# Other slots for the attention steps, a second output buffer in x1, identity products in the first block, and another order in the last block

## What is computed

```python
x = hidden_states
n = layernorm(x)
q, k, v = n @ Wq.T, n @ Wk.T, n @ Wv.T
# chunks of 64 rows: o = q @ state + tril(q @ k.T) @ v; state = state + k.T @ v
o = o / max(|sum(q * cumsum(k))|, 1)
o = rmsnorm(o) * norm_w
x = x + layernorm(o @ Wo)
n = layernorm(x)
w = routing(sigmoid(n @ Wr / temperature))     # zone weights, else the two nearest experts
y = sum over e of w[e] * ((silu(n @ Wg[e]) * (n @ Wu[e])) @ Wd[e])
out = x + layernorm(y)
```

## Time and profile before

| | |
|---|---|
| time, three runs | 1609.62, 1609.85, 1610.92 us; median 1609.85 |
| profiled execution | 1609.45 us, its span 1607.7 us |
| busy | PE 94%, DVE 62%, ACT 43%, POOL 28% |
| mean granted clock of TensorE | 0.983 |
| one pass of the loop | 96.2 us, from one wait of `kv 1` to the next |
| a store of 256 KB, from issue to landing | 2.2 us (median) |

### The profile page before, as it was taken

The page is one execution under the profiler, slowest core; times in us unless marked ns, Lnnn a source line. Parts: engine busy times, 40 slices in busy tenths (PEclk is TensorE's granted clock), DMA queues, the critical chain, the costliest instruction groups (busy, mean ns, idle before and its releaser), DMA issues. The chain is left out here.

```text
span 1607.7 us, 35519 instructions
## 1 busy us (share of the span) xinstructions
PE 1514.8 (94%) x13504; PEld 1299.3 (81%) x13504; DVE 989.7 (62%) x2388; ACT 692.4 (43%) x1264; POOL 456.4 (28%) x720
## 2 busy tenths in 40 slices
PE   5599999999999999999999999999999999999987
PEld 4488888788888888888788888888888888888876
DVE  5546666666665666656666665666656666665654
ACT  4443534444343443434444343443444445343432
POOL 1322413224241232413224241233413224241220
PEclk9599999999999999999999999999999999999999
DMA  3300000000000000000000000000000000000000
GB/s 113 98 2 3 25 0 13 13 13 13 0 13 13 13 13 12 14 0 13 13 13 13 0 13 13 13 13 13 13 0 13 13 13 13 0 13 15 1 14 13
DMA packets 25342, 24.54 MB, mean 15 GB/s; under 512 B 2016, under 2 KB 25056, under 8 KB 25312
## 3 DMA queue, kind: packets, MB, share of 16 engines
q1 hardware_dynamic: 25312, 24.13, 4.7%
HBM read 15.74 MB, written 8.39 MB: 15 GB/s over the span
## 5 line engine op out<-in xcount | busy, mean ns | idle before, releaser
L899 DVE TENSOR_TENSOR late<-late,up_ps 128x512 f32<-128x512 f32 x256 | 175.4, 685 | 317.7 <-PE up_ps L412 288.3
L412 PE MATMUL down_ps<-w_hi,h_hi 128*128 128x256 f32 x976 | 266.7, 295 | 0.0
L704 ACT ACTIVATE late<-gate_ps 128x512 f32<-128x512 f32 x256 | 152.7, 597 | 235.6 <-PE gate_ps L412 235.6
L412 PE MATMUL down_ps<-w_hi,h_lo 128*128 128x256 f32 x976 | 253.5, 281 | 0.0
L623 ACT ACTIVATE h_hi<-late 128x512 fp32r<-128x512 f32 x256 | 160.6, 627 | 203.5 <-DVE late L899 203.5
L1093 POOL TENSOR_TENSOR rms_f<-rms_in,minus_half 128x16 f32<-128x16 f32 x32 | 93.7, 2929 | 511.0 <-DVE rms_in L863 511.0
L919 DVE SCALAR_TENSOR_TENSOR late<-down_ps,route,late 128x256 f32<-128x256 f32 x364 | 158.1, 476 | 112.7 <-PE down_ps L412 109.2
L412 PE MATMUL gate_ps<-ft_hi,w_hi 128*128 128x512 f32 x512 | 211.3, 413 | 6.1 <-ACT late L704 5.3
L815 DVE TENSOR_TENSOR h_lo<-late,h_hi 128x512 fp32r<-128x512 f32 x256 | 175.2, 684 | 59.3 <-ACT h_hi L623 59.3
L412 PE MATMUL up_ps<-ft_hi,w_hi 128*128 128x512 f32 x512 | 204.2, 399 | 0.0
L412 PE MATMUL up_ps<-ft_hi,w_lo 128*128 128x512 f32 x512 | 204.0, 398 | 0.0
(11 more groups left out here) (154 smaller groups left out, 2638.1 us busy)
## 6 DMA issues: line engine op xcount, KB each, us to landing
xs<-in_x SPq DMA_DIRECT2D x32, 256.0 KB, 2.9
out_rows<-late SPq DMA_DIRECT2D x32, 256.0 KB, 2.2
late<-in_wg SPq DMA_DIRECT2D x8, 256.0 KB, 3.0
late<-in_wu SPq DMA_DIRECT2D x8, 256.0 KB, 2.8
late<-in_wd SPq DMA_DIRECT2D x8, 256.0 KB, 2.8
late<-in_wkv_t SPq DMA_DIRECT2D x1, 512.0 KB, 5.6
late<-in_wq_t SPq DMA_DIRECT2D x1, 256.0 KB, 4.4
late<-in_wo_t SPq DMA_DIRECT2D x1, 256.0 KB, 5.5
```

The source lines that it names most:

```text
L412: last = nc.tensor.matmul(dst, lhs, rhs, start=n == 0, stop=n == len(terms + low_terms) - 1)
L704: nc.scalar.activation(h_f[:, m, :], gate_ps[:, :], ACT.Silu).then_inc(silu_ready[0], 1)
L899: nc.vector.tensor_tensor(h_f[:, m, :], h_f[:, m, :], up_ps[m][:, :], ALU.mult).then_inc(h_ready[0], 1)
```

## The change

It moves steps among the slots of `STEPS`: `kv 1` from slot 5 to 3, `o 0` and `su 1` from 8 to 7, `norm_stats 0` from 9 to 8, `s 1` from 10 to 8, `norm_apply 0` from 11 to 10, `o 1` from 12 to 11, `ot 0` from 13 to 12, `ln2_apply 0` from 17 to 16, `ln2_add 0` and `ln3_stats 0` from 18 to 17, `ln2_stats 1` from 19 to 18, `ln3_apply 0` from 20 to 19, `ft 0` and `ln2_apply 1` from 21 to 20, `ln2_add 1` and `ln3_stats 1` from 22 to 21, `ln3_apply 1` from 24 to 23, `ft 1` from 25 to 24. The others stay. The second half's outputs go to a buffer of their own, which lies in `x1`. `normalise_x` signals each of its four tiles. In the first block TensorE makes products of the identity into `gate_ps` ahead of steps, and the order of the start on ScalarE and VectorE differs. In the last block `keep_x1`, `normalise_out` of the block before, the wait for its `out_add` and the last but one `add_down`s stand elsewhere.

```diff
--- before.py
+++ after.py
@@ -56,22 +56,21 @@
     [("xt", 0), ("xt", 1)],
     [("kv", 0)],
     [("q", 0), ("q", 1)],
-    [("kt", 0)],
+    [("kv", 1), ("kt", 0)],
     [("su", 0), ("s", 0)],
-    [("kv", 1), ("keep_x1",)],
+    [("keep_x1",)],
     [("kt", 1)],
+    [("o", 0), ("su", 1)],
+    [("norm_stats", 0), ("s", 1)],
     [],
-    [("o", 0), ("su", 1)],
-    [("norm_stats", 0)],
-    [("s", 1)],
     [("norm_apply", 0)],
     [("o", 1)],
-    [("ot", 0), ("norm_stats", 1)],
+    [("ot", 0)],
+    [("norm_stats", 1)],
     [("wo", 0)],
     [("norm_apply", 1), ("ln2_stats", 0)],
-    [("ot", 1)],
-    [("wo", 1), ("ln2_apply", 0)],
-    [("ln2_add", 0), ("ln3_stats", 0)],
+    [("ot", 1), ("ln2_apply", 0)],
+    [("wo", 1), ("ln2_add", 0), ("ln3_stats", 0)],
     [("ln2_stats", 1)],
     [("ln3_apply", 0)],
     [("ft", 0), ("ln2_apply", 1)],
@@ -79,6 +78,7 @@
     [],
     [("ln3_apply", 1)],
     [("ft", 1)],
+    [],
     [("ft_out", 0), ("ft_out", 1)],
     [],
 ]
@@ -109,6 +109,9 @@
     [("ft_out", 1)],
     [],
 ]
+
+FIRST_WARM = {("kv", 0): 4, ("s", 0): 1, ("kv", 1): 2, ("s", 1): 3, ("o", 1): 4, ("ot", 0): 4, ("wo", 0): 5, ("ot", 1): 5,
+              ("wo", 1): 4, ("ft", 0): 10, ("ft", 1): 14}
 ROUTER = ("r",)
 
 
@@ -159,11 +162,14 @@
         o_n = shared[:, :].rearrange("p (a b h d) -> p a b h d", a=2, b=2, h=H)
         fin = shared[:, :].rearrange("p (t n) -> p t n", t=TILES)
         state = sb("state", [P, B, 4, 2, HG * PAIR])
-        o_sb = sb("o_sb", [P, 2, H, VA])
+        o_sb0 = sb("o_sb0", [P, 2, H, VA])
         o_sq = sb("o_sq", [P, 2, H, VA])
 
         ot_hi, ot_lo = (xt[:, 0, :].rearrange("p (b n) -> p b n", b=B) for xt in (xt_hi, xt_lo))
         x1 = sb("x1", [P, TILES, HID])
+
+        o_sb = [o_sb0[:, :, :, :], x1[:, :, :].rearrange("p t n -> p (t n)")[:, 0:2 * H * VA]
+                .rearrange("p (b h v) -> p b h v", b=2, h=H)]
 
 
         ft_hi, ft_lo = sb("ft_hi", [P, KT, TOK], f32r), sb("ft_lo", [P, KT, TOK], f32r)
@@ -216,7 +222,7 @@
         x_loaded = counter("x_loaded", 32)
         out_stored = counter("out_stored", 32, 32)
         att_done = counter("att_done", N_PSUM)
-        xn_ready = counter("xn_ready", 1)
+        xn_ready = counter("xn_ready", TILES)
         xt_hi_ready = counter("xt_hi_ready", KT)
         xt_ready = counter("xt_ready", KT)
         q_ready = counter("q_ready", HG)
@@ -425,8 +431,11 @@
                     reach(pe, count, (a[0], a[1] - 1), k)
                 if kind == "xt":
                     k = step[1]
-                    reach(pe, xn_ready, a, 1)
                     for t in range(TILES):
+                        if psum_order(a) is FIRST_PSUM_STEPS:
+                            reach(pe, xn_ready, a, t + 1)
+                        elif t == 0:
+                            reach(pe, xn_ready, a, TILES)
                         last = nc.tensor.transpose(dst[:, t // 2, t % 2 * P:t % 2 * P + P], rows[:, t, k * P:k * P + P],
                                                    ident[:, :])
                 elif kind == "q":
@@ -488,7 +497,8 @@
                                                             start=False, stop=b == B - 1 and j == HPG - 1)
                 elif kind == "su":
                     p = step[1]
-                    reach(pe, v_ready, a, p + 1)
+                    if psum_order(a)[number - 2][0] != "kv":
+                        reach(pe, v_ready, a, p + 1)
                     pe.sem_inc(quarters_begun, 1)
                     for b in range(B):
                         for g in range(HG):
@@ -587,12 +597,23 @@
                 up(0, 1, a)
                 down(E - 1, 1, f)
 
+
+
+            def warm(count):
+                for _ in range(count):
+                    nc.tensor.matmul(gate_ps[:, 0:P], ident[:, :], ident[:, :], start=True, stop=True)
+
             pe.wait_ge(const_ready, 1)
+            warm(14)
             for n, steps in enumerate(FIRST_STEPS):
-                if n == 1:
-                    pe.wait_ge(w_ready, ATT_W)
                 for step in steps:
+                    warm(FIRST_WARM.get(step, 0))
+                    if step == ("kv", 0):
+                        pe.wait_ge(w_ready, 2)
+                    if step == ("wo", 0):
+                        pe.wait_ge(w_ready, ATT_W)
                     att_step(step, (0, 0))
+            warm(2)
             pe.wait_ge(w_ready, ATT_W + 3)
             up(0, 0, (0, 0))
             pe.wait_ge(wr_ready, 1)
@@ -631,7 +652,8 @@
                 return last
 
             def normalise_x(a):
-                ln_apply(1, 1, a, rows, xs, range(TILES), shift1, rstd1).then_inc(xn_ready[0], 1)
+                for t in range(TILES):
+                    ln_apply(1, 1, a, rows, xs, [t], shift1, rstd1).then_inc(xn_ready[0], 1)
 
             def normalise_out(p, f):
                 ln_apply(4, p + 1, f, fin, fin, range(2 * p, 2 * p + 2), shift4, rstd4).then_inc(fin_ready[0], 1)
@@ -656,14 +678,14 @@
                     last.then_inc(kz_ready[0], 1)
                 elif kind == "o":
                     p = step[1]
-                    reach(act, on_ready, a, p)
+                    reach(act, on_ready, a, p - 1)
                     for i in range(2):
-                        last = copy(o_sb[:, :, i * HPG:i * HPG + HPG, :],
+                        last = copy(o_sb[p][:, :, i * HPG:i * HPG + HPG, :],
                                     src[:, i, :].rearrange("p (b j v) -> p b j v", b=B, j=HPG))
                     last.then_inc(o_copied[0], 1)
                     reach(act, rms_in_ready, a, p)
                     reach(act, o_copied, a, p + 1)
-                    nc.scalar.activation(o_sq[:, :, :, :], o_sb[:, :, :, :], ACT.Square).then_inc(o_squared[0], 1)
+                    nc.scalar.activation(o_sq[:, :, :, :], o_sb[p], ACT.Square).then_inc(o_squared[0], 1)
                 elif kind == "ot":
                     copy(ot_hi, src).then_inc(ot_hi_ready[0], 1)
                 elif kind == "wo":
@@ -766,9 +788,11 @@
 
             act.wait_ge(att_w_loaded[0], 16)
             copy(wq_hi[:, :, :], wq_raw).then_inc(w_hi_ready, 1)
+            normalise_x((0, 0))
             act.wait_ge(att_w_loaded[1], 16)
             copy(wkv_hi[:, :, :], wkv_raw).then_inc(w_hi_ready, 1)
-            normalise_x((0, 0))
+            for step in FIRST_STEPS[0]:
+                att_step(step, (0, 0))
             act.wait_ge(wo_scaled, 1)
             copy(wo_hi[:, :, :], wo_raw).then_inc(w_hi_ready, 1)
             act.wait_ge(small_loaded, 48)
@@ -776,8 +800,9 @@
             copy(wr_h0[:, :, 0:E], wr_raw[:, :, :])
             nc.scalar.activation(wr_h0[:, :, E:2 * E], wr_raw[:, :, :], ACT.Copy, scale=0.0).then_inc(wr_hi_ready, 1)
             for n, steps in enumerate(FIRST_STEPS):
-                for step in steps:
-                    att_step(step, (0, 0))
+                if n > 0:
+                    for step in steps:
+                        att_step(step, (0, 0))
                 high_of_unit(n)
             act.wait_ge(temp_ready, 1)
             act.wait_ge(w_ready, ATT_W + UNITS - 2)
@@ -794,12 +819,15 @@
                 first_expert((i, 1), (i, 0), (i, -1))
             rest((BLOCKS - 1, 0), (BLOCKS - 2, 0), more=False)
             f = (BLOCKS - 1, 0)
-            first_expert(None, f, (BLOCKS - 2, 0))
-            keep_x1(f)
+            first_expert(None, f, None)
             for e in range(2, E):
                 for m in range(MT):
                     silu(e, m, f)
                     high(e, m, f)
+                if e in (3, 4):
+                    normalise_out(e - 3, (BLOCKS - 2, 0))
+                if e == 6:
+                    keep_x1(f)
             normalise_out(0, f)
             normalise_out(1, f)
 
@@ -865,7 +893,7 @@
                 elif kind == "norm_apply":
                     p = step[1]
                     reach(dve, rms_ready, a, p + 1)
-                    nc.vector.tensor_tensor(o_n[:, p, :, :, :], o_sb[:, :, :, 0:D],
+                    nc.vector.tensor_tensor(o_n[:, p, :, :, :], o_sb[p][:, :, :, 0:D],
                                             rms_f[:, p, :, :].unsqueeze(3).broadcast_to([P, B, H, D]), ALU.mult)\
                         .then_inc(on_ready[0], 1)
                 elif kind == "ot":
@@ -912,6 +940,8 @@
             def add_down(e, p, f):
                 if e == 1:
                     reach(dve, acc_scaled, f, p + 1)
+                if e == E - 1 and is_last(f):
+                    reach(dve, down_read, f, 2 * (e - 2) + p + 1)
                 reach(dve, down_done, f, 2 * e + p + 1)
                 for n in range(2):
                     t, src = 2 * p + n, down_bank(e, p, f)[:, n * HID:(n + 1) * HID]
@@ -970,15 +1000,17 @@
             x_stats((0, 0))
             nc.vector.memset(state[:, :, :, :, :], 0.0)
             settle(nc.vector.memset(v_sb[:, :, :, D:VA], 1.0))
+            dve.wait_ge(w_hi_ready, 1)
```

(17 more changed lines are left out.)

## The result

The changed kernel takes 1562.61 us (median of 4 runs, 1561.69 to 1563.77), the kernel before 1609.93 (4 runs, 1609.62 to 1610.92): a ratio of 0.9705, 95% interval 0.9689 to 0.9722. That is 47.3 us less; 45.4 were forecast.

A forecast was written before the change was run, and what follows sets the result against it. TensorE, busy 94% of the span, can gain only where it stands still or runs at half clock. Loop 33, first block 3 and last block 9 us sum to 45: 1609.85 - 45.4 = 1564.4, own range 1558 to 1570.

The forecast's parts named there:

- The stretch from `kt 1` to `down(1,1)`: Loop: a new TensorE wait of 1.0 to 1.2 us in each pass that finishes an output.
- the `state` wait: Loop: TensorE's wait ahead of kv 1 for DVE's state sums, 1.96 us from start to start, goes.
- Rival (b): Loop: no new wait replaces kv 1's, DVE or GpSimd being quicker than summed; 59 us gained, 1550; chance 0.14.
- `ft`: Loop: waits ahead of the two ft transposes shrink, 1.1 to 1.3 of 2 x 0.65 us gained a pass.
- rival (c): Loop: the new wait takes kv 1's whole gain, or ft keeps its waits; 1579, half way 1572; chance 0.24.
- The pass: Loop: one pass gains 2.3 us (2.0 to 2.5) and takes 93.9.
- Rival (d): Loop: slower, keep_x1 waiting on ScalarE for the store and delaying silu(2,1); 1627 if the store takes 10 us; chance 0.03.
- The first block: Block 1's predecessor: own output buffer and identity products gain 3 us, bounds 1 and 5.
- The buffer: First block: the o 1 copy and following square leave the way of ot 0's copy; about 1.1 us, bounds 0.7 and 1.7.
- The clock held through `up(0,0)`: First block: identity products may keep full clock, 2.9 us instead of 5.25, gaining 2.3; half was given.
- The 1.4 at `kv 0`: First block, kv 0: a further 1.4 us may come from the clock, at the same odds as at up(0,0).
- The last block: Last block: up(3,0) 7.5 us earlier, the tail 1.5 to 1.8; total 9.2, bounds 7.7 and 10.

The follow-up runs named there:

- `kv_only`: The changed kernel with the loop's slots of before, except kv 1 alone moved from slot 5 to slot 3: 1583.09 us, ratio 0.9841.
- `norm_first`: The changed kernel with ScalarE issuing normalise_out(1) ahead of the k and v copies of kv 1: 1548.49 us, ratio 0.9629.
- `no_products`: The changed kernel without any identity product: 1564.56 us, ratio 0.9736.
- `norm_early_last`: The changed kernel with the last block's normalise_out, and so out_add, back in first_expert, keep_x1 left at expert 6: 1562.95 us, one run.

## Why the prediction was right, step by step

**The stretch from `kt 1` to `down(1,1)`.** Forecast: the `state` wait goes (1.96) and a wait on `add_down(1,0)` of 1.0 to 1.2 comes, for 0.9 to 1.1 gained a pass. Measured: the new wait costs 1.05, and `kv_only` gains 12.6 us, 0.9 in each of 14 passes. `norm_first` shows the cause: with `normalise_out(1)` ahead the wait is gone and 14.7 us with it. Rival (b), no wait, is what that kernel does and the changed one doesn't. One number was written down wrong: DVE's wait for GpSimd was to grow to "near 3.5 or more", while the text's own shift (298.4 against 295.14, on top of 1.74) makes 5.0; 4.86 was measured.

**`ft`.** Forecast: 1.1 to 1.3 a pass, `ft 1` with nothing to spare. Measured: all waits gone in the loop, 20.3 us, 1.35 in each of the 15 blocks that have them. The doubt was too large: `ft 1` starts at 344.80 behind an `ln3_apply` that runs from 342.99 to 344.1, 0.7 to spare. With that, rival (c) falls. The pass came out at 94.0 (93.9 forecast).

**Rival (d), the store.** `keep_x1` waits 0.8 us at most in the loop, and nothing of it reaches TensorE. The price was rightly placed, though: in the last block, where no slack lies behind it, it was 68.4 - 62.5 = 5.9 us.

**The first block.** Forecast 3, measured 4.0: 0.9 up to `ft 1` and 3.2 from there to `xt`. The buffer gave its 1.1 between `ot 0` and `ot 1` (8.31 before, 7.22 after), of which 0.9 is left at `ft 1`. The clock held through `up(0,0)`, where I had given it even odds: 5.25 went to 2.87, all of the 2.3 forecast in that case; of the 3.2, 2.4 are the products' by `no_products` and 0.8 came without them. The 1.4 at `kv 0`, also at even odds, did not come in this profile: `kv 0` took 4.42 (4.20 before), while it took 2.9 in four of the nine profiles with products at the start. So the 3 was a mean of outcomes, and that the profile gave 4.0 is in part luck. The clock behind `ft 1` does not always hold either: in 3 of the 10 profiles with products ahead of it the stretch took 12.6 to 13.2 us instead of 11.4. It was 11.4 in all four in which TensorE stood 0.9 to 1.1 us ahead of `ft 1`, and in three of the six in which it stood 2.0 to 2.5. Ten profiles do not tell this from even odds.

**The last block.** Forecast 7.5 + 1.5 to 1.8; measured 7.9 + 1.4. Putting each edit back cost 5.9 (`keep_x1`), 1.5 (`normalise_out`) and 1.6 (`add_down`); 9.0 of the 9.3. The relief on DVE was sized too small: the sum went from 1545.1 to 1543.8, which is 1.3 for a relief of 0.9 to 1.6. Measured, `hidden(2,0)` can start 4.13 behind `down(1,0)` instead of 5.80, 1.67 sooner. The prediction had seen one slow route operation (1.05 to 0.19), and there were two: the `tensor_scalar` two places behind it took 0.88 before and 0.17 after. By the rule of the Trainium skill, "SBUF — State Buffer", section "Who interferes with whom", the whole 8.2 was to come; the measured 7.9 lies between that and the 7.5.

One reading was loose: the first slice in the earlier trace rows is a 9 like the 38 behind the second, so only the second stands out. Nothing was summed from it.

The medians differ by 47.3, the profiled spans by 46.2. What lies around the span is 1.75 in both profiled executions, so the 1.1 between is the spread from run to run.

## What to carry to other kernels

When a step moves to an earlier slot, read not only whether its own wait goes, but what each engine's queue now holds behind it: here ScalarE did two copies sooner and an output's normalisation 3.2 us later (287.30 - 282.19 behind the start of slot 3, before 291.93 - 290.04), and through GpSimd and VectorE that came back on TensorE as half of the gain. Once such a wait shows in the trace, follow its releaser back to the instruction that has no reason to be late, and put that one first: moving two lines was worth 14 us. A copy whose only wait is a store should stand where nothing urgent follows it on its engine. And before a small difference between two loops is put down to the clock, the granted clock has to be read over the whole of both: here the same 1.7 us lay in block 1 of one run and in block 2 of the other.

## What the runs showed of the hardware

- An identity product of 128x128x128 in float32 is recorded as two matmuls and takes 0.24 us at full clock (20 records in 2.39) and 0.41 where the clock was half for most of them (28 in 5.71).
- TensorE's clock came back to full during such a run of products, after a wait of 3.77 us and four transposes at half clock. Whether it stayed full until `xt`, and whether it fell behind it, changed from profile to profile with the same products ahead of `ft 1`.
- Beside one of GpSimd's additions of 128x512 float32 (1.28 to 1.29 us each) a VectorE operation of a few elements took as long as the addition still ran: in `norm_early_last` 1.06 us for a `tensor_tensor` of 128x32 (0.19 alone), ending 0.06 behind the addition, and 0.91 for a `tensor_scalar` with one input of 128x4 (0.17 alone), ending 0.02 behind the next. In the loop it is the one of 128x64, 1.23 (0.22 in the last block), where VectorE has time to spare. I had looked for the delay in the two-input operation only. The page "SBUF — State Buffer" of the Trainium skill, in "Who interferes with whom", counts `tensor_scalar` among the operations that can enter a mode that uses both ports, where it too contends with GpSimd; by that rule the row agrees, though no run here tells which mode the operation was in.
